# Graph layers with a running maximum: two columns a step fetched row by row into a buffer of their own, and ScalarE's projections between its portions of rows

## The reference

```python
def sage(x, src, dst, Wl, bl, Wr):
    agg = segment_max(x[src], dst, num_segments=x.shape[0])
    agg = where(isfinite(agg), agg, 0.0)
    return agg @ Wl + bl + x @ Wr
h = maximum(layernorm(x), 0)
h = leaky_relu(sage(h, src, dst, Wl1, bl1, Wr1), 0.01)   # 128 -> 256
h = leaky_relu(sage(h, src, dst, Wl2, bl2, Wr2), 0.01)   # 256 -> 256
h = leaky_relu(sage(h, src, dst, Wl3, bl3, Wr3), 0.01)   # 256 -> 128
out = x + h
```

## Time and profile before

| | |
|---|---|
| median of 3 runs | 6052.86 us (6050.67 to 6052.91) |
| the profiled execution | 6050.56 us |
| its span | 6048.9 us |
| POOL busy | 4524.8 us, 75% |
| DVE busy | 2893.5 us, 48% |
| ACT busy (without DMA issue) | 225.4 us, 4% |
| PE busy | 732.5 us, 12% |

### The profile page before, as it was taken

One profiled execution on the slowest core, in us unless ns is written; L12 is line 12 of the kernel. 1 busy time (PEld: TensorE's weight loads), 2 busy tenths in 40 slices (PEclk: granted clock), 3 DMA queues, 4 the chain that ended last, 5 costly groups with the idle time before them and its releaser, 6 DMA issues.

```text
span 6048.9 us, 53349 instructions
## 1 busy us (share of the span) xinstructions
PE 732.5 (12%) x2214; PEld 411.8 (7%) x2214; DVE 2893.5 (48%) x3638; ACT 225.4 (4%) x664; POOL 4524.8 (75%) x4793
## 2 busy tenths in 40 slices
PE   1111111111100311111111110040010000100003
PEld 0000000000000200000000000030000000000002
DVE  5333333333333555555555555565555555555556
ACT  1000000000000100000000000010000000000001
POOL 6777777777777777777777777767777777777776
PEclk7555555555555655555555555575555555555556
DMA  4333333333333566666666666666666666666665
GB/s 141 108 111 107 108 108 109 110 108 108 108 108 107 171 216 218 218 216 220 216 218 218 216 219 214 215 206 219 217 220 215 218 218 216 220 215 218 215 216 175
DMA packets 461123, 1089.10 MB, mean 180 GB/s; under 512 B 116295, under 2 KB 181740, under 8 KB 461068
## 3 DMA queue, kind: packets, MB, share of 16 engines
q0 software_dynamic: 203520, 519.10, 30.6%
q1 hardware_dynamic: 220508, 544.04, 24.8%
q10 hardware_dynamic: 37040, 25.45, 1.5%
HBM read 555.08 MB, written 533.07 MB: 180 GB/s over the span
## 4 chain that ended last, share of the span: by engine, by line
POOL 49%; issue 17%; DMA 1%; POOLq 1%; DVE 0%; PE 0%; DVEq 0%
POOL ring L448 47%; POOL ring L475 2%; POOLq L444 0%; DMA ring<-running_max_log,end_row 0%; POOLq L441 0%; DMA patch<-running_max_log,patch_row 0%; DMA ring<-features,stage 0%; DMA running_max_log<-patch 0%; POOL patch L465 0%; DVE z_sum L902 0%; DVE agg L894 0%; POOLq L455 0%; POOLq L443 0%; DMA features<-h_out 0%; DVE patch L873 0%
## 5 line engine op out<-in xcount | busy, mean ns | idle before, releaser
L448 POOL DMA_INDIRECT ring<-features,stage x4611 | 4360.0, 946 | 1432.2 <-issue 1383.7
L792 DVE TENSOR_TENSOR ring<-banks,ring 128x1024 f32<-128x1024 f32 (+1 forms) x1173 | 1227.4, 1046 | 2954.0 <-DMA ring<-features,stage 2918.9
L758 DVE TENSOR_TENSOR banks<-ring,banks 128x1024 f32<-128x1024 f32 (+1 forms) x1173 | 1232.1, 1050 | 37.5
L975 PE MATMUL banks<-wr,h_turned 128*128 128x256 f32 (+1 forms) x490 | 220.7, 596 | 3623.4 <-ACT h_turned L1109 3623.4
L975 PEld LDWEIGHTS banks<-wr,h_turned 128*128 128x128 f32 x490 | 127.2, 320 | 3687.4 <-ACT h_turned L1109 3678.6
L991 PE MATMUL banks<-dst_low,own 128*128 128x394 bf16 x200 | 100.4, 502 | 976.0 <-DVE own L734 976.0
L475 POOL DMA_INDIRECT ring<-running_max_log,end_row x147 | 142.9, 972 | 65.6 <-issue 43.9
L1109 ACT ACTIVATE h_turned<-banks 128x256 f32<-128x256 f32 (+1 forms) x147 | 51.8, 353 | 3128.6 <-issue 2664.1
L739 DVE COPY stage<-edges 128x8 int32 (+1 forms) x588 | 119.4, 203 | 88.0 <-DVE banks L758 32.8
L977 PE MATMUL banks<-b,ones 1*128 1x256 f32 (+1 forms) x294 | 157.6, 637 | 0.0
L1048 PE MATMUL banks<-wl,agg 128*128 128x256 f32 (+1 forms) x490 | 110.7, 369 | 1.2 <-DVE agg L894 0.9
(11 more groups left out here) (114 smaller groups left out, 523.4 us busy)
## 6 DMA issues: line engine op xcount, KB each, us to landing
running_max_log<-ring SPq DMA_DIRECT2D x782, 512.0 KB, 3.1
running_max_log<-ring SPq DMA_DIRECT2D x391, 256.0 KB, 2.2
ring<-features ACTq DMA_DIRECT2D x4752, 1.0 KB
ring<-features,stage POOLq DMA_INDIRECT x4611, 3.2
ring<-features SPq DMA_DIRECT2D x3888, 1.0 KB
ring<-features ACTq DMA_DIRECT2D x2376, 0.5 KB
ring<-features SPq DMA_DIRECT2D x1944, 0.5 KB
h_in<-features ACTq DMA_DIRECT2D x98, 128.0 KB, 2.5
```

Of the source, the lines that this page charges most:

```text
L448: pool.indirect_dma_start(ring[0:rows, c * w:(c + 1) * w], None, tables[l], bass.IndirectOffsetOnAxis(ap=stage[0:rows, b, u:u + 1].bitcast ...
L758: dve.tensor_tensor(sum_ps[:, 0:CHAINS * w].rearrange("p (h f) -> p h f", h=CHAINS), group(g - 1).rearrange("p (h f) -> p h f", h=CHAINS), ...
L792: dve.tensor_tensor(group(g), sum_ps[:, 0:CHAINS * w], group(g), ALU.max).then_inc(turn, 1)
L975: pe.matmul(mm_ps[p][:, 0:n], h_turned[p][:, c, :], wr_sb[l][:, c, :], start=(c == 0), stop=False)
```

## The change

Every full step now has two whole columns, 54 and 55, fetched row by row: 256 rows, 128 by SP in portions of 16 and 128 by ACT in portions of 32. They go into a buffer of their own, `fetched`, not into the ring. POOL fetches 54 whole columns. At group 13 DVE takes two maxima of two columns each, one with the ring's own columns and one with `fetched`, and waits for the rows only between them. Rows may start once DVE has added group 0 of the step (`block_scanned`), with no wait for a log store. SP stores whole blocks (8 columns) in full steps, and issues two portions of rows behind each store. In the wide layers ACT copies and keeps its two tiles between its four portions; in the first layer, and in steps without tiles, it does the portions together, as before.

```diff
-SYNC_ROWS, SYNC_AT_ONCE = 72, 8
-ACT_AT_ONCE = 11
-ROWS = 160
+FETCHED_COLS = 2
+SYNC_ROWS = 128
+AT_ONCE, ACT_AT_ONCE = 16, 32
...
+    ROWS = FETCHED_COLS * P
...
-        return width(b, last) - (b == BLOCKS - 1 and not last)
+        return width(b, last) - (FETCHED_COLS if b == BLOCKS - 1 and not last else 0)
...
-    STORES_OF = [width(b, False) // CHAINS for b in range(BLOCKS)]
+    STORES_OF = [1 for b in range(BLOCKS)]
...
+        fetched = sb("fetched", [P, FETCHED_COLS * F_MAX])
...
-            before, p = divmod(ROWS_OF[k][0] + r, P)
-            c = RING_COLS - 1 - before
-            p += before * (2 * P - ROWS)
-            return ring[p:p + 1, c * w:(c + 1) * w].bitcast(U8)
+            ahead, p = divmod(ROWS_OF[k][0] + r, P)
+            c = FETCHED_COLS - 1 - ahead
+            return fetched[p:p + 1, c * w:(c + 1) * w].bitcast(U8)
...
-                        elif g == GROUPS - 1:
+                        dve.wait_ge(turn, carried + 2 * g + 1)
+                        if g == GROUPS - 1:
+                            gathered = (CHAINS - FETCHED_COLS) * w
+                            dve.tensor_tensor(group(g)[:, 0:gathered], sum_ps[:, 0:gathered], group(g)[:, 0:gathered],
+                                              ALU.max).then_inc(turn, 1)
                             dve.wait_ge(act_rows_landed, FETCHED[1])
                             dve.sem_inc(act_rows_landed, -FETCHED[1])
                             dve.wait_ge(sync_rows_landed, FETCHED[0])
                             dve.sem_inc(sync_rows_landed, -FETCHED[0])
-                        dve.wait_ge(turn, carried + 2 * g + 1)
-                        dve.tensor_tensor(group(g), sum_ps[:, 0:CHAINS * w], group(g), ALU.max).then_inc(turn, 1)
+                            dve.tensor_tensor(group(g)[:, gathered:CHAINS * w], sum_ps[:, gathered:CHAINS * w],
+                                              fetched[:, 0:FETCHED_COLS * w], ALU.max).then_inc(turn, 1)
+                        else:
+                            dve.tensor_tensor(group(g), sum_ps[:, 0:CHAINS * w], group(g), ALU.max).then_inc(turn, 1)
...
+                def rows_open(i):
+
+                    if isinstance(i, int):
+                        act.wait_ge(rows_placed, len(widths))
+                    act.wait_ge(block_scanned, i * BLOCKS + (SIGNED * l + BLOCKS))
...
+                def step_of_rows(i, pair):
+
+                    rows_open(i)
+                    if pair and l:
+                        for p in range(2):
+                            fetch_rows(i, range(2 * p, 2 * p + 1))
+                            keep_turned(i, p, True)
+                            fetch_rows(i, range(2 * p + 1, 2 * p + 2))
+                            keep_own(i, p)
+                    else:
+                        fetch_rows(i, range(ACT_PORTIONS))
+                        if pair:
+                            keep_pair(i, 2)
...
+                        sp.wait_ge(block_scanned, i * BLOCKS + (SIGNED * l + BLOCKS))
+                        fetch_rows(i, portion)
+                        portion += 1
                     for b in used_blocks(last):
...
-                        if columns > CHAINS:
+                        if last and columns > CHAINS:
...
-                        at = columns - CHAINS
-                        sp.dma_start(log_block(l, i, b, at, CHAINS), ring[:, (c + at) * w:(c + columns) * w]
+                        at = columns - CHAINS if last else 0
+                        sp.dma_start(log_block(l, i, b, at, columns - at), ring[:, (c + at) * w:(c + columns) * w]
                                      ).then_inc(logged[b], DMA)
-                        if not last and (BLOCK_GROUPS * b + 1) * SYNC_AT_ONCE < SYNC_ROWS:
-                            fetch_rows(i, BLOCK_GROUPS * b + 1)
+                        for portion in range(portion, min(portion + PORTIONS, portions)):
+                            fetch_rows(i, portion)
+                        portion += 1
```

More of the change, by code:

```diff
@@ L23 @@
 BLOCK_GROUPS = BLOCK_COLS // CHAINS
-TURNS = 2 * GROUPS + 1
+TURNS = 2 * GROUPS + 2
 STORES = 5
@@ L307, in run_neighbours, with lists_of @@
             return pairs
-        def list_of(edges_src):
-            pairs = []
-            for first, count, run in ((0, P, (CHAINS - 1) * P), (P, ROWS - P, (CHAINS - 1) * P - (ROWS - P))):
-                chain = run * RUN + GROUPS - 1
-                pairs.append((row_list[:, first:first + count],
-                              bass.AP(edges_src.tensor, chain, [[GROUPS, STEPS - 1], [RUN, count]])))
-            return pairs
+        def lists_of(edges_src):
+            return [(row_list[:, k * P:(k + 1) * P],
+                     bass.AP(edges_src.tensor, (CHAINS - 1 - k) * P * RUN + GROUPS - 1, [[GROUPS, STEPS - 1], [RUN, P]]))
+                    for k in range(FETCHED_COLS)]
         def row_places(k, engine, i, at, count, w):
@@ L414, in _ @@
                         pool.dma_start(dest, there).then_inc(sort_done, DMA)
-                pool.wait_ge(list_loaded, 2 * DMA)
+                pool.wait_ge(list_loaded, FETCHED_COLS * DMA)
                 with nc.allow_non_contiguous_dma(reason="one word of each row to fetch"):
-                    for here, there in list_of(sorted_src):
+                    for here, there in lists_of(sorted_src):
                         pool.dma_start(here, there).then_inc(sort_done, DMA)
@@ L446, in gather @@
                             c = b * BLOCK_COLS + u
-                            rows = 2 * P - ROWS if c == RING_COLS - 2 and not last else P
                             pool.indirect_dma_start(
-                                ring[0:rows, c * w:(c + 1) * w], None, tables[l],
+                                ring[:, c * w:(c + 1) * w], None, tables[l],
                                 bass.IndirectOffsetOnAxis(
-                                    ap=stage[0:rows, b, u:u + 1].bitcast(U32), axis=0),
+                                    ap=stage[:, b, u:u + 1].bitcast(U32), axis=0),
                             ).then_inc(late_landed if last and b == LATE_BLOCK and u >= CHAINS else landed[b], DMA)
@@ L689, in _ @@
             dve.memset(restart_turns[:, :, 0], LOWEST).then_inc(prep_done, 1)
-            dve.wait_ge(list_loaded, 2 * DMA)
+            dve.wait_ge(list_loaded, FETCHED_COLS * DMA)
             for w in widths:
@@ L1141, in keep_pair, with fetch_rows @@
                         keep_own(j, p)
-                def fetch_rows(i):
-                    act.wait_ge(group_scanned, i * BLOCKS + (FIRSTS * l + 1))
+                def rows_open(i):
                     if isinstance(i, int):
                         act.wait_ge(rows_placed, len(widths))
-                        if l:
-                            act.wait_ge(logged[BLOCKS - 1], LOGGED[BLOCKS - 1] * l)
-                    else:
-                        act.wait_ge(logged[BLOCKS - 1], i * (DMA * STORES_OF[BLOCKS - 1]) + LOGGED[BLOCKS - 1] * l)
-                    for first in range(0, ROWS_OF[1][1], ACT_AT_ONCE):
+                    act.wait_ge(block_scanned, i * BLOCKS + (SIGNED * l + BLOCKS))
+                def fetch_rows(i, portions):
+                    for portion in portions:
+                        first = portion * ACT_AT_ONCE
                         places = row_places(1, mybir.EngineType.Activation, i, first, ACT_AT_ONCE, w)
@@ L1207, in _ @@
             with nc.allow_non_contiguous_dma(reason="one word of each row to fetch"):
-                for here, there in list_of(src):
+                for here, there in lists_of(src):
                     sp.dma_start(here, there).then_inc(list_loaded, DMA)
@@ L1213, in _, with fetch_rows, log_step @@
             for l, (w, n) in enumerate(shapes):
-                def fetch_rows(i, g):
-                    first = g * SYNC_AT_ONCE
-                    if g == 0:
+                def fetch_rows(i, portion):
+                    first = portion * AT_ONCE
+                    places = row_places(0, mybir.EngineType.SP, i, first, AT_ONCE, w)
+                    for r, place in enumerate(places):
+                        sp.dma_start(row_slot(0, first + r, w), table_row(l, w, place)
+                                     ).then_inc(sync_rows_landed, DMA)
+                def log_step(i, last):
+                    portion, portions = 0, 0 if last else SYNC_ROWS // AT_ONCE
+                    if not last:
                         if isinstance(i, int):
```

29 lines of the change are left out of this document (10 added, 19 removed).

## The result

The changed kernel takes **6178.48 us** (median of 4 runs, 6172.88 to 6184.47), the kernel before 6052.89 us beside it: a ratio of 1.0209, 95% interval 1.0191 to 1.0226. It is 126 us slower, where 96 us faster was predicted, and outside the range.

A forecast was written before the change was run, and what follows sets the result against it. POOL's gathers, 1.25 us each, were taken as the bound. The profiled 6050.6 us, less 101.3 for removed gathers, plus 5 for row waits, gave 5954; the median lies 2.3 above, so 5957 us, range 5944 to 6160 (8 in 10).

The forecast's parts named there:

- the sum's first term: POOL's chain: one gather fewer in each of 81 full steps, at 1.25 us each, 101.3 us off.
- 27 C + 35 against 27 x 68.8 + 65: A layer of 27 steps with row cycle C is as long as before when both sides are equal, at C = 69.9.
- SP 67.8: SP's cycle of rows in wide layers, 51.0 us plus eight address loads of 2.1, beside POOL's 67.5.
- h_in's row: Landing of the last single row in the cycle, taken from the nearest profile row, h_in's: 2.5 us for 128 KB.
- The load, 2.1 us for 16 words: SP's address load for a portion of 16 rows in wide layers, estimated at 2.1 us; eight a step.
- flat and proportional growth: Address load time against words: for SP's 16 in wide layers 1.40 us if flat, 2.8 if proportional.
- no growth, 1.40: Low end for SP's 16-word address load: as long as the eight-word load in wide layers, 1.40 us.
- rival 2: SP's eight address loads a step in wide layers become the bound, deciding from 2.44 us each; 6208 at 2.8; chance 0.15.
- Whole-block stores: nothing: SP's 1 MB stores land in at most 6.2 us, POOL wants the block some 50 us after its scan: no cost.
- Rival 3: Rows get in each other's way: ACT's at 0.42 us instead of 0.36 make its cycle 73.2, time 6197; chance 0.11.
- busy but not full: If single rows all go to one DMA engine, its share is 0.66 + 0.15 = 0.81, leaving the sum unchanged.
- the sign that I named for this rival: A long pitch of the single rows would show that they get in each other's way.

The follow-up runs named there:

- everything earlier: Changed kernel with SP's address loads ahead of block stores, each step's first load and SP's first 16 rows earlier, 60 idle SP instructions added: 6097.86 us, ratio 1.0075.
- half gathers: Changed kernel with SP's address loads ahead of block stores, and wide-layer gathers fetching 512 of 1024 bytes: 6051.52 us, ratio 1.0001.

## Why the prediction was wrong

**What held.** POOL was the bound before, one gather costs 1.25 us, and a step of 54 takes 67.5 us once nothing else is longer: the first layer has it, and the version with 224 rows, which leaves out 32, has it everywhere, at 5955 us beside the predicted 5957. So the sum's first term was right. ACT's tiles between its portions cost nothing. Even the rule for a layer's length (27 C + 35 against 27 x 68.8 + 65) holds: with C = 72.7 it gives +75 us for each wide layer and -34 for the first, +116, and +126 was measured.

**"SP 67.8".** This is the step that failed. The measured 72.7 is 4.9 above it, in three of its terms, by their averages over the 20 steps. Up to the first row I had 5.0 us (DVE 2.3, a store 0.6, a load 2.1), and it is 6.9. From the first row's issue to the last's I had 60.3 (67.8 without those 5.0 and the landing's 2.5), and it is 61.6. For the landing I took the 2.5 us of h_in's row, and it is 4.3.

**The load, 2.1 us for 16 words.** I chose between flat and proportional growth, and it is neither: the same 16 words take 1.2 or 3.2 us by what stands ahead of them in the queue. The low end that I gave as "no growth, 1.40" was too high for the fast kind. The mean is what matters: in SP's single records the eight loads of a wide step sum to 19.8 us on average, 2.5 each, past rival 2's own point of decision at 2.44. For 32 words I took 3.3, and it is 2.2. The Trainium skill's rule of about 200 ns a register ("Runtime: NRT & Kernel Launch", section "Instruction fetch mechanics"), with its 6.4 us for 32, does not hold here: it is 68 ns a word for 32, and 75 for SP's 16 behind rows. Right behind a 1 MB store SP's 16 words do come to 200 ns each (3.2 us).

**"Whole-block stores: nothing".** I priced them at POOL, which wants the block 50 us later, and there they do cost nothing (1.0007). What they hold up is the queue behind them, which I priced from the start of a *half* block's store: 1.96 us to the next row became 3.69. Five places a step have it. Nor do they land in at most 6.2 us: it is 7.1 on the page.

**Rival 3, "busy but not full".** I had the mechanism, and dismissed it with 10 us of packets in 67.5 beside a mean share of 0.68. That count is half of what it should be. ACT's queue moved 37040 packets with 88 rows a step and moves 43520 with 128, so a row is (43520 - 37040)/(81 x 40) = 2 packets, and 256 rows are 20 us. By the rule quoted there (the Trainium skill, "DMA: Bandwidth & Descriptors", section "Why a DMA increments its semaphore by 16 and not by 1") the one engine would then have been at 0.66 + 0.30 = 0.96, nearly full, where I had 0.81. The rows of the changed kernel:

```profile
q10 hardware_dynamic: 43520, 28.23, 1.7%
...
2200.00:3700.00 1500.00, 157.45 (x328) 80.34 (x328) 739.14 (x769) 31.41 (x82) 1067.31 (x1129) 0.50 0.63 208
```

They give 39 ns a packet and a mean share of 0.63, so the same estimate makes 0.88 of it. It makes 0.90 of 256 rows with everything earlier (period 71.3) and 0.90 of 224 (67.5), but only 0.76 of 256 rows beside half gathers (70.3), which still land 5.0 us late. So the time of packets explains a part and not all. One server for rows of both queues fits the rule, but no view names the engine, so that it is this engine stays argued, not shown. And the sign that I named for this rival, a longer pitch of the rows, did not come: ACT's 32 rows take 11.9 to 12.4 us in the step above, 0.37 to 0.39 each, where I took 0.36 and the rival's case was 0.42. The delay is in the landing.

**Two rivals as one.** I gave the two mechanisms chances of their own, each with the other absent. They are neighbours: whichever is relieved, the step falls by 0.2 or 1.2 us onto the other, and only both give 3.7. That the prices of the two (6208 and 6197) lie near the measured 6178 is luck: each put the whole excess into one term, all eight loads at 2.8 us or the pitch of ACT's rows. The chance that both stand within 5 us of the bound had no place in my list.

**Open.** What exactly the server's time for a row is: 66 us for 256 rows when they begin late, 69 when they begin early, about 2 less with half the gathers' bytes. No single rate fits these. Why a load is slow while block stores are issued, and grows with its words, stays open too.

## What to carry to other kernels

Where two chains run within a few microseconds of the bound, relieving one shows next to nothing; remove both in one run before calling either innocent. Price an instruction in a queue by what will stand right ahead of it after the change, not by its mean before. Count what one transfer puts on an engine (two packets a row here) before calling the engine busy but not full. Single-row transfers have a capacity of their own: watch how long after the last issue the waiting engine starts, and whether that grows over a step.

## What the hardware showed unexpectedly

- A load of 16 words takes 1.2 us, or 3.2 right behind a 1 MB store on the same queue, and one of 8 words 0.7 or 1.5. One of 32 words takes 2.2 us, but 7.5 where it starts while another queue issues the last of three such stores.
- Single rows of both queues share something that in the wide layers keeps up with 224 in 67.5 us, but not with 256. Rows of 64 bytes in place of 1024 shorten the step of 72.7 us by 0.4, or that of 72.5 by 0.7. In the first layer, with half the bytes everywhere, it keeps up with 256.
- A row sent as two pieces takes 25.04/32 = 0.78 us of its queue, a load's share included, where a whole one takes 11.80/32 = 0.37.
- A loop body of 302 recorded instructions on SP stalls 5.1 us at each branch back or not at all, by where it lies: 6203 and 6098 us with the same work. The packets on the instruction queue (305 and 65) tell which.
